# Two VectorE operands of layer 1 read from PSUM instead of SBUF

## The chip, the cores and the metric

The kernel runs on one core of one Trainium2 chip. The metric is the device time of one execution in microseconds. Five engines run side by side, each through its own list of instructions in order: TensorE (PE), VectorE (DVE), ScalarE (ACT), GpSimd (POOL) and SyncE (SP). They meet only at semaphores. TensorE writes its results to PSUM, which has eight banks of 512 fp32 values in each of 128 partitions; VectorE and ScalarE read and write PSUM and SBUF.

## What is computed

A graph with 6250 nodes (256 values each) and 100000 edges goes through two layers. Layer 0 sends a message along each edge, sums the messages by node and updates the node by a gate; a layer norm follows. Layer 1 is graph attention with 8 heads:

```python
    s_u = x @ W_u.T + b_u
    s_v = x @ W_v.T
    e = s_u[src] + s_v[dst]
    e = jnp.where(e >= 0, e, 0.2 * e)
    m = jax.ops.segment_max(e, dst, num_segments=n_nodes)
    e_exp = jnp.exp(e - m[dst])
    denom = jax.ops.segment_sum(e_exp, dst, num_segments=n_nodes)
    probs = e_exp / denom[dst]
    xh = x.reshape(n_nodes, head_dim, num_heads)
    msg = xh[src] * probs[:, None, :]
    out = jax.ops.segment_sum(msg, dst, num_segments=n_nodes)
```

The edges come sorted by `dst`. A second layer norm ends the computation.

## The kernel before

The kernel has five stages, one after the other: setup (some 320 us), layer 0 (to about 2900 us), the node update (to about 3200 us), layer 1 (to about 4845 us) and the output. The change lies in layer 1 alone, the function `layer1_phase`.

Layer 1 lays the edges out in 880 tiles of 128 edges, one edge to a partition, and takes them in 55 groups of 16 tiles (`GROUP` = 16). Two buffer sets (`SETS` = 2, index `r`) alternate. For group `g` the steps are these:

- GpSimd gathers the rows of the 16 tiles with 16 indirect DMAs (L1466), each of 128 rows of 264 fp32 values (`XW`: 256 features and 8 scores), into `feats[r]`. Their row numbers stand in `gsrc[r]` in SBUF. Before a group's gathers GpSimd waits for `index_ready`, and before each four of them until the sums that use the buffer are done (`agg_done`).
- VectorE forms the scores when all 16 gathers have landed and the sums of the group before are added (`take_scores`, L1589 to L1592), and then a running maximum along the edges (`local_max`, L1598 to L1601). Its last instruction in the body of a group is `stage_index` (L1574), which writes the row numbers of the group after the next into `gsrc[r]` and so releases that group's gathers.
- In the body of the next group VectorE first makes the one-hot tile of the nodes (`find_node`, L1578), chains the maxima over the tiles (L1659 to L1670), and compares in `find_edge` (L1581) a row of column numbers, `K["column"]`, broadcast over 16 tiles, with each edge's place, `loX`, broadcast over 128 columns. The result is `same`, 128 by 2048 values, the matrix that TensorE sums with. After two scans (L1679, L1680) and a turn on TensorE comes `below`, the score less its maximum (L1688).
- ScalarE takes the exponential of `below` (L1564) and writes the 8 weights of each edge into the last 8 columns of its row of `feats[r]`, where TensorE sums them with the features.
- VectorE multiplies the features by the weights in four quarters, in place (L1699). TensorE multiplies `same` with `feats` for two tiles at a time into `psU` (L1532), and VectorE adds each of the eight results to `acc` in SBUF (`add_sums`, L1611).

The order of each engine's work is written out by hand. On VectorE the body of a group is: L1578, the chain of maxima, L1581, the scans, L1688, L1693 (`acc` by a factor), two quarters of L1699 and the sums between and after the other two, then `take_scores` and `local_max` of the group after it, then L1574. In PSUM the stage has seven tensors of one bank each: `psE`, `psM`, `psV` and four `psU`. Layer 0 has the same kinds of work in other shapes: gathers at L918, scatters at L935, a comparison of two SBUF tensors at L1071, and at L1122 a sum of a PSUM tensor and an SBUF tensor.

## Time and profile before

| | us |
|---|---|
| median of 3 runs | 4930.07 (4929.89 to 4938.38) |
| the profiled execution | 4929.81 |
| its span in the trace | 4928.1 |
| POOL busy in the span | 3434.9 (70%) |
| PE busy | 3099.3 (63%) |
| DVE busy | 2202.6 (45%) |
| ACT busy | 908.4 (18%) |

The page gives the busy time in 40 slices of the span, one digit for each, in tenths:

```profile
PE   3547877777777777877778768834444444444441
DVE  2543333333333333333333349855555555555554
POOL 4238888888888888888888867756666666666564
PEclk9869898888998888888898889956666666666665
```

The last 14 slices are layer 1 and the output. No engine is full there: GpSimd is busy six tenths of the time, VectorE five, TensorE four.

### The profile page before, as it was taken

The numbers are of one execution on the slowest core, as the hardware profiler recorded it, in microseconds if no ns is written. First come the engines' busy times: TensorE is split into PE (matmuls) and PEld (weight loads), VectorE is DVE, ScalarE is ACT, GpSimd is POOL, SyncE is SP. The second block draws the span as 40 slices with busy tenths as digits, with TensorE's granted clock in tenths as the row PEclk, the third lists the DMA queues.
The fourth block names the chain that finished last, engine by engine and source line by source line (L and its number), as shares of the span: only waits on it lengthen the run. The fifth ranks groups of instructions, "written<-read, shape, count | busy, mean of one in ns | idle before, by whom it ended". The sixth has DMA issues, their size and how long they took to land. (4 is left out here: it accounts for less than half of the span.)

```text
span 4928.1 us, 61408 instructions
## 1 busy us (share of the span) xinstructions
PE 3099.3 (63%) x13554; PEld 1900.6 (39%) x13555; DVE 2202.6 (45%) x5019; ACT 908.4 (18%) x2810; POOL 3434.9 (70%) x2948
## 2 busy tenths in 40 slices
PE   3547877777777777877778768834444444444441
PEld 1224444444444444444444435523333333333331
DVE  2543333333333333333333349855555555555554
ACT  0212222222222222222222223300000000000002
POOL 4238888888888888888888867756666666666564
PEclk9869898888998888888898889956666666666665
DMA  7777767667767677677677666643333333333332
GB/s 285 193 241 137 135 126 136 133 123 135 132 126 138 127 131 134 126 135 132 123 136 132 123 133 206 181 148 93 95 92 100 93 94 91 96 98 94 92 93 66
DMA packets 471760, 641.52 MB, mean 130 GB/s; under 512 B 173608, under 2 KB 365636, under 8 KB 467887
## 3 DMA queue, kind: packets, MB, share of 16 engines
q0 software_dynamic: 198144, 339.26, 36.4%
q1 hardware_dynamic: 245994, 254.83, 17.6%
q10 hardware_dynamic: 27588, 47.08, 3.0%
q8 instruction: 10, 0.16, 0.0%
q14 instruction: 24, 0.19, 0.0%
HBM read 448.23 MB, written 192.71 MB: 130 GB/s over the span
## 5 line engine op out<-in xcount | busy, mean ns | idle before, releaser
L935 POOL DMA_INDIRECT S<-l_msum,l_sink x784 | 1280.7, 1634 | 254.2 <-issue 213.5
L1466 POOL DMA_INDIRECT l_feats<-X_rows,l_gsrc x880 | 1008.1, 1146 | 605.6 <-DVE l_gsrc L1574 340.7
L918 POOL DMA_INDIRECT l_ga<-A_rows,l_gsrc x784 | 791.3, 1009 | 265.6 <-issue 155.4
L1008 PE MATMUL l_psU<-l_hid,l_same 128*128 128x257 f32 x1568 | 585.0, 458 | 534.7 <-ACT l_hid L1044 518.2
L981 PE MATMUL l_psC<-l_table,l_onehot 128*128 x4728 | 726.5, 295 | 0.0
L1532 PE MATMUL l_psU<-l_feats,l_same 128*128 128x264 f32 x1760 | 555.7, 481 | 146.5 <-DVE l_feats L1699 129.2
L1048 ACT COPY l_msum<-l_psU 128x257 f32<-128x257 f32 x784 | 292.6, 373 | 1883.8 <-POOLq L934 1296.1
L974 PE MATMUL l_psC<-W1cT,l_attrT 64*128 64x256 f32 x1576 | 619.0, 476 | 13.1 <-DMA l_table<-B_rows 13.1
L981 PEld LDWEIGHTS l_psC<-l_table,l_onehot 128*128 128x128 bf16 x4728 | 426.0, 104 | 364.9 <-issue 303.4
L1008 PEld LDWEIGHTS l_psU<-l_hid,l_same 128*128 128x128 f32 x1568 | 266.1, 213 | 669.9 <-ACT l_hid L1044 598.9
L1532 PEld LDWEIGHTS l_psU<-l_feats,l_same 128*128 128x128 f32 x1760 | 413.8, 242 | 281.8 <-issue 189.2
L1122 DVE TENSOR_TENSOR l_hidden<-l_psG,bgate 128x256 f32<-128x256 f32 x147 | 62.4, 425 | 824.8 <-PE l_psG L1023 673.4
L974 PEld LDWEIGHTS l_psC<-W1cT,l_attrT 64*128 64x128 f32 x1576 | 260.3, 206 | 267.4 <-issue 230.7
L1080 DVE TENSOR_SCALAR l_togo<-srcT,spare 128x8 f32 x98 | 25.7, 262 | 694.9 <-POOLq L934 626.2
L1044 ACT ACTIVATE l_hid<-l_ga 128x256 f32<-128x256 f32 x784 | 331.0, 422 | 0.0
L1097 DVE TENSOR_TENSOR l_ga<-l_ga,l_psC 128x256 f32<-128x256 f32 x784 | 308.5, 415 | 45.0 <-PE l_psC L981 20.8
L1501 PE MATMUL l_psE<-ident,l_score 128*128 128x128 f32 x55 | 25.9, 471 | 435.4 <-DVE l_score L1592 435.4
L1611 DVE TENSOR_TENSOR acc<-acc,l_psU 128x264 f32 x440 | 188.4, 428 | 237.7 <-PE l_psU L1532 144.1
L1699 DVE TENSOR_TENSOR l_feats<-l_feats 128x1024 f32<-128x1024 f32 x220 | 264.0, 1221 | 4.2 <-DVE acc L1693 0.5
L1562 ACT ACTIVATE l_shrink<-l_psE 128x8 f32<-128x8 f32 x55 | 9.7, 177 | 1223.6 <-PE l_psE L1519 1042.8
L1023 PE MATMUL l_psG<-WhhT,l_xgT 128*128 128x256 f32 x588 | 195.4, 417 | 0.0
L1501 PEld LDWEIGHTS l_psE<-ident,l_score 128*128 128x128 f32 x55 | 9.9, 180 | 457.9 <-DVE l_score L1592 457.9
(346 smaller groups left out, 3512.2 us busy)
## 6 DMA issues: line engine op xcount, KB each, us to landing
l_srcb<-src_rows SPq DMA_DIRECT2D x99, 512.0 KB
l_locb<-lo_rows SPq DMA_DIRECT2D x55, 512.0 KB
S<-su_zeros ACTq DMA_DIRECT2D x24, 1156.5 KB
l_locb<-loc_rows SPq DMA_DIRECT2D x99, 256.0 KB
nd_sums<-S SPq DMA_DIRECT2D x196, 128.5 KB, 2.2
l_attr<-in_edge_attr SPq DMA_DIRECT2D x98, 256.0 KB
GH_rows<-l_hidden SPq DMA_DIRECT2D x49, 384.0 KB
nd_hidden<-GH_rows SPq DMA_DIRECT2D x49, 384.0 KB, 3.2
```

The costliest lines, as they stand in the source:

```text
L918: pool.indirect_dma_start(ga[:, s, :], None, D["A"], bass.IndirectOffsetOnAxis(ap=gsrc[h][:, j % HALF:j % HALF + 1], axis=0)).then_inc(gat ...
L935: pool.indirect_dma_start(D[f"S{j % NTAB}"], bass.IndirectOffsetOnAxis(ap=sink[j // HALF][:, j % HALF:j % HALF + 1], axis=0), msum[:, j % ...
L974: nc.tensor.matmul(pc(j), attrT[j // 4 % 2][side, j % 4 // 2 * P:(j % 4 // 2 + 1) * P], K["W1cT"][side, :], start=True, stop=False)
L981: t = nc.tensor.matmul(pc(j), onehot[j // HALF % 2][:, w, j % HALF, :], flat(table[:, bass.ds(blocks[j % 4] + w, 1), n * H:(n + 1) * H]), ...
L1008: nc.tensor.matmul(psU[j % 2][:, 0:UW], same[j // HALF][:, j % HALF, :], hid[:, j % RING, :], start=True, stop=True).then_inc(agg_done, 1)
L1023: t = nc.tensor.matmul(psG[:, 0:H], xgT[:, k * P:(k + 1) * P], K["WhhT"][:, k, n * H:(n + 1) * H], start=(k == 0), stop=(k == HC - 1))
L1044: nc.scalar.activation(hid[:, j % RING, 0:H], ga[:, j % SLOTS, :], ACT.Relu).then_inc(hid_ready, 1)
L1048: nc.scalar.copy(msum[:, j % RING, :], psU[j % 2][:, 0:UW]).then_inc(msum_ready, 1)
L1097: nc.vector.tensor_tensor(ga[:, s, :], ga[:, s, :], pc(j), ALU.add).then_inc(pre_ready, 1)
L1466: pool.indirect_dma_start(feats[r][:, t, :], None, D["X1"], bass.IndirectOffsetOnAxis(ap=gsrc[r][:, t:t + 1], axis=0)).then_inc(gathered[r ...
L1532: i = nc.tensor.matmul(psU[n % 4][:, 0:XW], same[:, t, :], feats[r][:, t, :], start=(t % PAIR == 0), stop=(t % PAIR == PAIR - 1))
L1699: nc.vector.tensor_tensor(f3, f3, w3, ALU.mult).then_inc(weighted, 1)
```

## The change

A new PSUM tensor `psW` takes the eighth bank. Two things lie in it. The first 128 columns, `weight`, hold the weights of a group, and the next 128, `column`, hold the row of column numbers, copied there once before the loop. `find_edge` reads its first operand from `column` in PSUM; its second, `loX`, stays in SBUF. ScalarE takes the exponential twice: first into `weight` (which signals `weights_ready`), then into the rows of `feats` as before (which signals the new semaphore `weights_in_rows`). VectorE's four products read the weights from PSUM and the features from SBUF. TensorE waits for `weights_in_rows` before the group's sums. The place of `stage_index` is the same as before, last in the body.

```diff
--- before.py
+++ after.py
@@ -1388,6 +1388,7 @@
         psE = m.ps("psE", [P, 512])
         psM = m.ps("psM", [P, 512])
         psV = m.ps("psV", [P, 512])
+        psW = m.ps("psW", [P, 512])
         psU = [m.ps(f"psU{q}", [P, 512]) for q in range(4)]
         keys_in, tables_ready, table_split = m.sem("keys_in"), m.sem("tables_ready"), m.sem("table_split")
         loc_in = [m.sem(f"loc_in{r}") for r in range(SETS)]
@@ -1399,12 +1400,14 @@
         ends_ready, ends_turned = m.sem("ends_ready"), m.sem("ends_turned")
         carries_ready, carries_turned, shrink_ready = m.sem("carries_ready"), m.sem("carries_turned"), m.sem("shrink_ready")
         max_ready, max_turned = m.sem("max_ready"), m.sem("max_turned")
-        below_ready, weights_ready = m.sem("below_ready"), m.sem("weights_ready")
+        below_ready, weights_ready, weights_in_rows = m.sem("below_ready"), m.sem("weights_ready"), m.sem("weights_in_rows")
         weighted, agg_done, acc_done = m.sem("weighted"), m.sem("agg_done"), m.sem("acc_done")
         dve_step, pool_waited = m.sem("dve_step"), m.sem("pool_waited")
         block = st.enter_context(nc.Block())
 
         ENDS, CARRY, SHRINK = P, P + 2 * GROUP, P
+        weight = psW[:, 0:GROUP * NH].rearrange("p (t h) -> p t h", h=NH)
+        column = psW[:, P:2 * P]
 
         def groups(engine, body):
 
@@ -1522,6 +1525,7 @@
                 pe.wait_ge(max_ready, g + 1)
                 nc.tensor.transpose(psM[:, 0:P], top[:, :], K["ident"][:, :]).then_inc(max_turned, 1)
                 pe.wait_ge(same_ready, g + 1)
+                pe.wait_ge(weights_in_rows, g + 1)
                 for n in range(PAIRS):
                     if n % 2 == 0:
                         pe.wait_ge(weighted, g * 4 + (n // 2 + 1))
@@ -1561,7 +1565,8 @@
                 act.wait_ge(carries_turned, g + 1)
                 nc.scalar.activation(shrink[:, :], psE[:, SHRINK:SHRINK + NH], ACT.Exp).then_inc(shrink_ready, 1)
                 act.wait_ge(below_ready, g + 1)
-                nc.scalar.activation(feats[r][:, :, H:XW], below[:, :, :], ACT.Exp).then_inc(weights_ready, 1)
+                nc.scalar.activation(weight, below[:, :, :], ACT.Exp).then_inc(weights_ready, 1)
+                nc.scalar.activation(feats[r][:, :, H:XW], below[:, :, :], ACT.Exp).then_inc(weights_in_rows, 1)
                 if not isinstance(g, int) or g < XG - SETS:
                     act.wait_ge(sv_done, g + 1)
                     stage_window(g + SETS, r)
@@ -1578,7 +1583,7 @@
                 nc.vector.tensor_scalar(onehot[:, :, :], locb[r][:, :, :], K["winid"][:, 0:1], None, ALU.is_equal).then_inc(onehot_ready, 1)
 
             def find_edge(g):
-                nc.vector.tensor_tensor(same[:, :, :], K["column"][:, :].unsqueeze(1).to_broadcast([P, GROUP, P]),
+                nc.vector.tensor_tensor(same[:, :, :], column.unsqueeze(1).to_broadcast([P, GROUP, P]),
                                         K["loX"][:, bass.ds(g * GROUP, GROUP)].unsqueeze(2).to_broadcast([P, GROUP, P]),
                                         ALU.is_equal).then_inc(same_ready, 1)
 
@@ -1627,6 +1632,7 @@
             split_float(nc, first_steps, K["svf"][:, :, :], svrest[:, :, :],
                         [table[:, :, n * NH:(n + 1) * NH] for n in range(NSPLIT)])
             dve.sem_inc(table_split, 1)
+            nc.vector.tensor_copy(column, K["column"][:, :])
             nc.vector.memset(ones[:, :], 1.0)
             nc.vector.memset(forth[:, 0:1], LOW)
             nc.vector.memset(carry[:, 1, GROUP - 1:GROUP], LOW)
@@ -1693,9 +1699,8 @@
                     c.link(nc.vector.tensor_tensor(rows, rows, factor[:, :].unsqueeze(1).to_broadcast([P, XW // NH, NH]), ALU.mult))
                 dve.wait_ge(weights_ready, g + 1)
                 for q in range(4):
-                    f = feats[r][:, q * QUARTER:(q + 1) * QUARTER, :]
-                    f3 = f[:, :, 0:H].rearrange("p t (c h) -> p t c h", h=NH)
-                    w3 = f[:, :, H:XW].unsqueeze(2).to_broadcast([P, QUARTER, H // NH, NH])
+                    f3 = feats[r][:, q * QUARTER:(q + 1) * QUARTER, 0:H].rearrange("p t (c h) -> p t c h", h=NH)
+                    w3 = weight[:, q * QUARTER:(q + 1) * QUARTER, :].unsqueeze(2).to_broadcast([P, QUARTER, H // NH, NH])
                     nc.vector.tensor_tensor(f3, f3, w3, ALU.mult).then_inc(weighted, 1)
                     if q == 1 or q == 2:
                         add_sums(g, (2 * q - 2, 2 * q - 1), blocks, first)
```

## Rows read from the trace of the kernel before

**Rows 1.** The waits of 3300 to 4800 us: who waited, for whom, total us, times, longest.
```profile
DVE l_score L1589 <- DMA l_feats<-X_rows,l_gsrc: 308.5, 52, 7.9
POOL l_feats L1466 <- DVE l_gsrc L1574: 304.9, 52, 6.1
```

**Rows 2.** The gathers of layer 1 by their line (ns min/median/max), and their row of the page.
```profile
L1466 POOL DMA_INDIRECT l_feats<-X_rows,l_gsrc x880: 940/946/3010, 3214.5 to 4820.3; - x176
...
L1466 POOL DMA_INDIRECT l_feats<-X_rows,l_gsrc x880 | 1008.1, 1146 | 605.6 <-DVE l_gsrc L1574 340.7
```

**Rows 3.** The timeline of one group: start us, duration us, engine, line, idle before it.
```profile
4010.09 0.17 DVE L1574 CAST l_gsrc<-srcX 128x16 int32 x1
...
4011.18 1.02 POOL L1466 DMA_INDIRECT l_feats<-X_rows,l_gsrc  x1 [5.84 <-DVE l_gsrc L1574]
...
4013.09 2.27 DVE L1581 TENSOR_TENSOR l_same<-column,loX 128x2048 f32<-128x2048 f32 x1
...
4013.75 2.44 POOL L1466 DMA_INDIRECT l_feats<-X_rows,l_gsrc  x1 [0.30 <-issue]
...
4017.68 0.29 DVE L1688 TENSOR_TENSOR l_below<-l_score,l_psM 128x128 f32<-128x128 f32 x1 [0.77 <-PE l_psM L1523]
4017.78 0.94 POOL L1466 DMA_INDIRECT l_feats<-X_rows,l_gsrc  x1 [0.31 <-issue]
...
4018.00 0.31 ACT L1564 ACTIVATE l_feats<-l_below 128x128 f32<-128x128 f32 x1 [3.28 <-DVE l_below L1688]
4018.41 2.36 DVE L1699 TENSOR_TENSOR l_feats<-l_feats 128x1024 f32<-128x1024 f32 x2
...
4019.03 1.43 POOL L1466 DMA_INDIRECT l_feats<-X_rows,l_gsrc  x1 [0.30 <-issue]
...
4021.93 0.43 DVE L1611 TENSOR_TENSOR acc<-acc,l_psU 128x264 f32 x1 [1.16 <-issue]
4022.01 0.95 POOL L1466 DMA_INDIRECT l_feats<-X_rows,l_gsrc  x1 [0.30 <-issue]
...
4036.14 0.56 DVE L1589 TENSOR_REDUCE l_score<-l_psV 128x128 f32<-128x384 f32 x1 [4.95 <-DMA l_feats<-X_rows,l_gsrc]
```

**Rows 4.** Busy time of two bursts of 16 gathers: the second one and one later.
```profile
core 0: us, PE busy (x) PEld busy (x) DVE busy (x) ACT busy (x) POOL busy (x), PEclk, DMA share, GB/s
3235.67:3255.38 19.71, 0.58 (x16) 0.51 (x16) 10.84 (x1) 4.46 (x17) 15.11 (x16) 0.50 0.88 280
4011.15:4034.18 23.03, 12.86 (x53) 9.70 (x53) 13.74 (x29) 1.99 (x10) 18.43 (x16) 0.65 0.40 113
```

**Rows 5.** Timeline: the first and the last comparison with a gather under it.
```profile
3285.24 2.27 DVE L1581 TENSOR_TENSOR l_same<-column,loX 128x2048 f32<-128x2048 f32 x1
...
3285.44 2.88 POOL L1466 DMA_INDIRECT l_feats<-X_rows,l_gsrc  x1 [0.30 <-issue]
...
4799.05 2.27 DVE L1581 TENSOR_TENSOR l_same<-column,loX 128x2048 f32<-128x2048 f32 x1
4799.18 2.97 POOL L1466 DMA_INDIRECT l_feats<-X_rows,l_gsrc  x1 [0.30 <-issue]
```

**Rows 6.** Timeline of layer 0: L1122, a gather under it; then all gathers of L918 (min/median/max).
```profile
2284.39 0.42 DVE L1122 TENSOR_TENSOR l_hidden<-l_psG,bgate 128x256 f32<-128x256 f32 x1 [4.58 <-PE l_psG L1023]
2284.61 0.99 POOL L918 DMA_INDIRECT l_ga<-A_rows,l_gsrc  x1 [0.30 <-ACT l_msum L1048]
...
L918 POOL DMA_INDIRECT l_ga<-A_rows,l_gsrc x784: 942/987/1980, 322.8 to 2864.2; - x196
```

**Rows 7.** VectorE groups by line, 3300 to 4800 us, and one line of the nodes stage.
```profile
L1699 DVE TENSOR_TENSOR l_feats<-l_feats 128x1024 f32<-128x1024 f32 x204 | 244.8, 1221 | 3.2
L1611 DVE TENSOR_TENSOR acc<-acc,l_psU 128x264 f32 x411 | 175.9, 428 | 222.2 <-PE l_psU L1532 130.6 <-issue 69.6 <-DVE acc L1611 21.5
...
L1693 DVE TENSOR_TENSOR acc<-acc,l_factor 128x264 f32 x51 | 22.1, 434 | 0.0
...
L1308 DVE TENSOR_TENSOR nd_rz<-nd_psRZ,nd_addend x49: 677/681/692, 2919.8 to 3197.5; 128x512 f32<-128x512 f32 x49
```

**Rows 8.** Timeline of GpSimd alone: the pause after the first gather of a burst.
```profile
4043.25 1.41 POOL L1466 DMA_INDIRECT l_feats<-X_rows,l_gsrc  x1 [2.25 <-issue]
```

## The prediction

> **What bounds the kernel now.** The change touches layer 1 alone, so I read the waits of that stretch first. Two waits answer each other there: VectorE waits for the gathers (308.5 us before L1589), and GpSimd waits for the row numbers of L1574 (304.9 us) [rows 1]. So the stage is one ring. GpSimd issues 16 gathers, the last one lands, VectorE forms the scores and the local maxima and writes the next row numbers, and GpSimd starts again. The timeline of one group shows GpSimd idle for 5.84 us between two bursts, and VectorE idle for 4.95 us until the burst has landed, with all its own work on the group done [rows 3]. Neither engine is full, but each us that a burst grows is a us of the ring. The wait for `agg_done` inside a burst never holds: the pauses between gathers are 0.30 us almost everywhere [rows 3].
>
> Next the burst itself. The smallest gather takes 940 ns and the median 946 ns, but the mean is 1146 ns and the longest 3010 ns [rows 2]. The second burst ran while VectorE did nothing with two SBUF tensors. It held 15.11 us of gathers in 19.71 us, which is 16 times 0.945 and 15 pauses. A later burst held 18.43 us of gathers in 23.03 us: all of its extra 3.3 us lies inside gathers [rows 4]. Summed over the 880 gathers, 1008.1 - 880 x 0.946 = 175.6 us lie above the median [rows 2]. That is the pot from which the change can take.
>
> The timelines show when a gather grows. One that started 0.66 us after the comparison L1581 took 2.44 us and ended 0.83 us after it. The first and the last such gather took 2.88 and 2.97 us and ended 0.81 and 0.83 us after the comparison [rows 3, 5]. One that started under the first of two products (L1699, 2.36 us for the two) took 1.43 us and ended 0.83 us after the first [rows 3]. So a gather that starts while such an instruction runs is held near its beginning, until the instruction has ended. Under L1611 (`acc` from SBUF, `psU` from PSUM, result to SBUF) a gather that started 0.08 us in took 0.95 us, and under L1688 (`score` from SBUF, `psM` from PSUM) one took 0.94 us [rows 3]. L1581 and L1699 read two tensors from SBUF; L1611 and L1688 read one. All bursts look alike: going through the 880 gathers in the timeline, I count 53 that start under L1581, with 67.5 us above the median together, and 136 that are held by L1699, with 97.5 us. None of those that start under L1611 or L1688 is above it. The other 10.6 us lie under setup work, under L1578, L1659 and L1680 (0.04 us at each of the 53 starts under it), and in scatter.
>
> **The change part by part.**
>
> *Removed: the hold under L1699.* After the change it reads features from SBUF and weights from PSUM, which is the form of L1611. Gain 97.5 us by the rows of L1611, nothing if PSUM did not help. I take 97.5.
>
> *Removed: the hold under L1581.* Here the first operand moves to PSUM and the second stays in SBUF. The nearest row is L1122 of layer 0, first operand `psG`, second an SBUF tensor. A gather that started 0.22 us into it took 0.99 us, and 987 ns is the median of all L918 gathers [rows 6]. So the order of operands does not matter, though L1122 is short (0.42 us). Gain 67.5 us; nothing at the other end. I take 67.5.
>
> *Moved reads: the length of the two VectorE instructions.* No row shows a product of 1024 or a comparison of 2048 values with a PSUM operand. L1611 takes 428 ns for 264 values, and L1693, the same size with both inputs in SBUF, 434 ns; L1308, first operand in PSUM and second in SBUF, takes 681 ns for 512 [rows 7]. From L1611 to L1308 that is 253 ns for 248 values, the rate of L1699 (1221 ns for 1024). I take the same length. The bounds are a few ns less and twice the time per value, which is rival three.
>
> By the Trainium skill (VectorE: DVE Perf Modes, The TRN2 errata) a PSUM source costs 120 cycles against 58 at 0.96 GHz. That would be 0.06 us more for each of five instructions of a group, 0.3 us that VectorE's idle time covers, and the pair of L1611 and L1693 does not show it [rows 7].
>
> *Added on ScalarE: a second exponential of each group.* It takes 0.31 us as L1564 does [rows 3]; written to PSUM, the first could take 0.05 us less or more, since no row shows ScalarE writing there. Products wait for the first alone. L1564 runs beside L1693, which ends at about the same time, so VectorE sees nothing of a small difference. The second ends some 0.35 us later, under the first product (1.22 us), and TensorE waits for that product anyway: cost zero, or 0.3 us of TensorE per group without that cover, which is not in the ring either. Behind the second exponential ScalarE's window copies (L1552) move by 0.35 us. They serve the group after the next, a whole period later. Cost zero.
>
> *Added: the wait for `weights_in_rows` on TensorE.* Queued behind it are the sums, which `weighted` holds for longer. Zero. *Added: one copy of 128 columns before the loop,* under 0.3 us. No DMA, no SP work and no GpSimd instruction is added or moved, and L1574 stays where it is.
>
> *What is late next.* VectorE idles 308.5 / 52 = 5.9 us per group before L1589 [rows 1]. The bursts shrink by 165 / 53 = 3.1 us each, so 2.8 us stay on average, and 4.95 - 3.3 = 1.6 us in the group shown. GpSimd still sets the pace: each us taken from a burst arrives.
>
> *New holds.* With the long holds gone, starts fall at fixed 1.25 us steps from the start of the burst, and may meet the short instructions that still read two SBUF tensors. By the group shown none meets L1693, whose 0.43 us would cost at most 0.43 - 0.12 = 0.31 us. The scan L1680 is met now already, for 0.04 us. If both were met at their start in all 53 groups it would cost 53 x (0.31 + 0.36) = 35 us.
>
> *Sum.* The profiled execution took 4929.81 us, its span 4928.1, and the median of the runs is 4930.07, so the three agree. 4929.8 - 97.5 - 67.5 = 4764.8 us.
>
> **The rivals.**
>
> *One: the comparison keeps its hold,* because its second operand still comes from SBUF. Then 4929.8 - 97.5 = 4832 us. Against it: L1122 [rows 6]. For it: L1122 is short, and such starts are few.
>
> *Two: nothing is given back.* The hold would hang on the length of the instruction or on its writing to SBUF, not on its second input. Then 4930 us. Against it: L1611 writes to SBUF and holds nothing [rows 3]. By the Trainium skill (SBUF — State Buffer, Who interferes with whom) an earlier probe saw no stall of GpSimd's DMAs under `tensor_tensor`, since descriptor generation is inferred to need the write interface only, and that would give this case; the same section says that two SBUF inputs contend with a GpSimd instruction that reads SBUF. The trace bears out the second: gathers of 2.44 us under L1581 [rows 3].
>
> *Three, the other side: PSUM operands stream at half rate,* as broadcast operands that are read again and again. Then L1581 grows by 2.13 us and the four products by 4 x 1.07 = 4.27 us, 6.4 us on VectorE per group. The ring passes to VectorE from 2.8 us on, and the kernel is slower from 5.9 us on. 53 x (6.4 - 5.9) = 27 us: 4957 us. Against it: L1611 and L1308 [rows 7], though neither broadcasts its PSUM operand.
>
> *Four: only the products slow down so.* 4.27 - 2.8 = 1.5 us per group, 53 x 1.5 = 78 us: 4843 us. VectorE is then the bound.
>
> **How the numbers follow.** Forecast 0.80, rival one 0.07, two 0.05, three 0.04, four 0.04. The forecast's range: upward 35 us of new holds, to 4800. Downward the whole pot, 175.6 us, and the pause of 2.25 us in place of 0.30 that 8 of the bursts have after their first gather [rows 8], 8 x 1.95 = 16 us, if that too hangs on VectorE: 4738. So 4740 to 4800 holds 0.80. Faster by over 0.2% (about 10 us, what a measurement of this kernel can tell from no change): 0.80 + 0.07 + 0.04 = 0.91. Within it 0.05, slower 0.04.
>
> **What would show it.** Gathers of L1466 in layer 1 at a mean near 0.96 us instead of 1.146, the longest under 1.5 us, and the mean period of a group near 26.0 us (29.1 less 3.1), where the 52 steps from the first to the last comparison give (4799.05 - 3285.24) / 52 = 29.1 [rows 5]. VectorE's wait before L1589 near 2.8 us per group and still ended by the gathers' DMA. L1581 at 2.27 us and the product at 1.22 us. Wrong would be: gathers still near 2.4 us under L1581 (rival one), L1581 above 3 us (three), or VectorE without idle time before L1589 (four).

## The result and the profile after

The changed kernel is slower: 5139.52 us median (5128.53 to 5145.09, four runs) against 4930.58 us (4929.89 to 4938.38) before, a ratio of 1.0415 with a 95% interval from 1.0396 to 1.0433. The forecast was 4764.8 us. The profiled execution took 5128.53 us and its span is 5126.8 us, so that is the time to explain: 198.7 us more than before.

The page of the changed kernel: its 40 slices, two of its DMA queues, and three rows of its costliest groups (out<-in, count | busy us, mean ns | idle us before).

```profile
PE   2657778787777778787777687344444444444441
...
DVE  3543333333333333333333398554544554555445
...
POOL 3248888888888888888888677444444444444444
PEclk9878988888888888888988899556666666666665
...
q8 instruction: 10, 0.16, 0.0%
q14 instruction: 23, 0.19, 0.0%
...
L1469 POOL DMA_INDIRECT l_feats<-X_rows,l_gsrc x880 | 837.5, 952 | 971.1 <-DVE l_gsrc L1579 706.0
...
L1616 DVE TENSOR_TENSOR acc<-acc,l_psU 128x264 f32 x440 | 188.5, 428 | 751.7 <-DMA B_rows<-su_zeros 317.3
...
L1704 DVE TENSOR_TENSOR l_feats<-l_feats,l_psW 128x1024 f32<-128x1024 f32 x220 | 263.0, 1216 | 2.3 <-ACT l_psW L1568 0.3
```

Layer 1's loop has grown longer, so it fills more slices, and in these VectorE is at 0.4 to 0.5. The gathers are as forecast: 837.5 us where there were 1008.1 [rows 2], a mean of 952 ns. Their line and that of the comparison (ns min/median/max) say the same:

```profile
L1469 POOL DMA_INDIRECT l_feats<-X_rows,l_gsrc x880: 943/949/1372, 3214.7 to 5015.3; - x176
...
L1586 DVE TENSOR_TENSOR l_same<-l_psW,loX x55: 2271/2292/2293, 3264.5 to 5026.6; 128x2048 f32<-128x2048 f32 x55
```

The median gather is as before and the longest takes 1372 ns in place of 3010 [rows 2]. The comparison takes 2292 ns and the product 1216 ns, as they did before [rows 3, 7]. Everything that the change was to do, it did. The gain of 170.6 us in the gathers is there, and the kernel is 199 us slower. The waits of the 52 steps (3300 to 5000 us) show where:

```profile
POOL l_feats L1469 <- DVE l_gsrc L1579: 669.2, 52, 14.1
...
PE l_psU L1536 <- DVE l_feats L1704: 422.8, 105, 9.3
DVE acc L1616 <- DMA B_rows<-su_zeros: 312.5, 64, 8.0
DVE acc L1616 <- PE l_psU L1536: 264.0, 140, 6.0
...
DVE acc L1616 <- issue: 128.0, 78, 7.4
...
PE l_psU L1536 <- issue: 100.1, 31, 5.6
```

GpSimd used to wait 304.9 us for the row numbers [rows 1], 5.9 us for each group. It now waits 669.2 us, 12.9 for each. VectorE's wait for the gathers' DMA before the score reduction (308.5 us in rows 1) is gone: after the start of the loop, L1594 waits for nothing. So the ring's slack is used up, and VectorE sets the pace. Its own idle time has moved to L1616, the addition of the sums, and the releasers that stand there make no sense: `su_zeros` belongs to a stage long over, and "issue" means that the profile knows of nothing to wait for. The timeline of one group (start us, duration us, engine, line, idle before it) shows what happens:

```profile
4009.21 0.95 POOL L1469 DMA_INDIRECT l_feats<-X_rows,l_gsrc  x1 [13.19 <-DVE l_gsrc L1579]
...
4017.37 6.35 PE L1536 MATMUL l_psU<-l_feats,l_same 128*128 128x264 f32 x16 [2.49 <-DVE l_feats L1704]
...
4019.53 0.43 DVE L1616 TENSOR_TENSOR acc<-acc,l_psU 128x264 f32 x1 [1.16 <-issue]
...
4027.32 0.43 DVE L1616 TENSOR_TENSOR acc<-acc,l_psU 128x264 f32 x1 [7.35 <-issue]
4027.66 1.21 DVE L1704 TENSOR_TENSOR l_feats<-l_feats,l_psW 128x1024 f32<-128x1024 f32 x1
4028.01 0.95 POOL L1469 DMA_INDIRECT l_feats<-X_rows,l_gsrc  x1 [0.30 <-issue]
...
4029.00 3.88 PE L1536 MATMUL l_psU<-l_feats,l_same 128*128 128x264 f32 x8 [5.28 <-DVE l_feats L1704]
4032.24 0.43 DVE L1616 TENSOR_TENSOR acc<-acc,l_psU 128x264 f32 x1 [3.36 <-PE l_psU L1536]
...
4040.99 1.02 POOL L1469 DMA_INDIRECT l_feats<-X_rows,l_gsrc  x1 [12.02 <-DVE l_gsrc L1579]
```

The burst begins at 4009.21. At 4019.53 VectorE adds the first pair of sums, and then it does nothing for 7.35 us. The block of 16 matmuls that began at 4017.37 holds four pairs of sums, and TensorE finished the second at 4021.25. Nothing that the program asks for is missing, and yet the next addition starts at 4027.32. The third product follows it at 4027.66, so TensorE, which needs that product, has idled for 5.28 us when it goes on at 4029.00; VectorE adds again at 4032.24, after 3.36 us, although this pair too lay in the block that ended at 4023.72. That is 23.03 us after the burst began, and from there on nothing is late. The last gather started at 4028.01. The row numbers come so late that the next burst starts at 4040.99, after 12.02 us of waiting where there were 5.84 [rows 3].

To count this in every kernel the same way I take, for each addition of a pair, its start less the later of two ends: that of VectorE's instruction before it, and that of TensorE's last matmul of the pair. Where this is above 1 us it is a *stall*. Before: none. After: 102, with 461.5 us, among 440 additions. The last stall of a group ends 23.0 us after the burst began in nearly every group.

VectorE is not alone. The register steps of the loop on ScalarE (ACTq) and SyncE (SPq), which wait for no semaphore, take this long (ns min/median/max):

```profile
L1556 ACTq FUSED_REGOPS  x440: 3/138/1422, 3239.5 to 4972.7; - x147
...
L1427 SPq FUSED_REGOPS  x26: 55/700/728, 3218.8 to 4875.0; - x26
```

From 3300 us on, no register step of either engine in the kernel before took 0.5 us or more; here some 250 do, nearly all of them 0.7 us, mostly at 1.40 us from one to the next. TensorE is touched too: where it had idled ahead of its sums for no known reason for 2.4 us in all, it now does so for 100.1 us, 5.6 us at the longest. And it runs its sums at a lower clock.

The kernel before shows the same on ScalarE once, in the second burst of the stage, where VectorE did nothing with two SBUF tensors and so no gather was held [rows 4]. ScalarE's register steps (one line, whole execution) and its copies in that burst:

```profile
L1552 ACTq FUSED_REGOPS  x440: 15/132/704, 3238.8 to 4776.2; - x147
...
3248.07 0.21 ACT L1552 COPY l_window<-l_table 128x24 bf16 x1 [3.92 <-issue]
3248.20 0.95 POOL L1466 DMA_INDIRECT l_feats<-X_rows,l_gsrc  x1 [0.30 <-issue]
3249.45 0.95 POOL L1466 DMA_INDIRECT l_feats<-X_rows,l_gsrc  x1 [0.30 <-issue]
3249.47 0.21 ACT L1552 COPY l_window<-l_table 128x24 bf16 x1 [1.19 <-issue]
...
3250.87 0.21 ACT L1552 COPY l_window<-l_table 128x24 bf16 x1 [1.19 <-issue]
```

These copies come at 1.40 us, and ahead of each stands a step of ScalarE's sequencer of 0.69 or 0.70 us. Seven such steps of L1552 lie between 3242 and 3256 us. No tensor of the change exists in that kernel.

The windows of one block of the changed kernel's sums and of the stage (busy us of PE, PEld, DVE, ACT and POOL, granted clock, DMA share, GB/s):

```profile
4017.40:4023.70 6.30, 6.30 (x16) 4.63 (x16) 1.40 (x2) 0.80 (x4) 4.77 (x6) 0.59 0.52 147
3300.00:4800.00 1500.00, 689.86 (x2549) 485.74 (x2548) 756.22 (x1644) 100.50 (x495) 690.47 (x726) 0.63 0.29 83
```

While these 16 matmuls ran the granted clock was 0.59 of full speed, where the sums of the group in rows 3 had 0.72 between 4019.8 and 4030.5 us. Over the stage it is 0.63 against 0.66. These are mixtures of the engine's two levels, 1.2 and 2.4 GHz; ahead of this block TensorE had idled for 2.49 us. The mean matmul of the sums, within 3300 to 4800 us, went from 481 to 558 ns.

### The profile page after: what moved, and what is told of

It is laid out like the page before. It is cut to its first block and busy times, and to the rows that moved or that the text cites. A ratio compares the mean times of both kernels' runs of the same rounds, so it can differ in the third digit from the quotient of the medians.

```text
span 5126.8 us, 61518 instructions
## 1 busy us (share of the span) xinstructions
PE 3213.0 (63%) x13554; PEld 1965.6 (38%) x13555; DVE 2208.0 (43%) x5020; ACT 922.0 (18%) x2865; POOL 3265.5 (64%) x2948
## 5 line engine op out<-in xcount | busy, mean ns | idle before, releaser
L1469 POOL DMA_INDIRECT l_feats<-X_rows,l_gsrc x880 | 837.5, 952 | 971.1 <-DVE l_gsrc L1579 706.0
L1536 PE MATMUL l_psU<-l_feats,l_same 128*128 128x264 f32 x1760 | 670.5, 554 | 535.6 <-DVE l_feats L1704 429.9
L918 POOL DMA_INDIRECT l_ga<-A_rows,l_gsrc x784 | 791.9, 1010 | 265.7 <-issue 162.2
L1536 PEld LDWEIGHTS l_psU<-l_feats,l_same 128*128 128x128 f32 x1760 | 477.4, 281 | 709.0 <-issue 575.7
L1616 DVE TENSOR_TENSOR acc<-acc,l_psU 128x264 f32 x440 | 188.5, 428 | 751.7 <-DMA B_rows<-su_zeros 317.3
L1122 DVE TENSOR_TENSOR l_hidden<-l_psG,bgate 128x256 f32<-128x256 f32 x147 | 62.5, 425 | 824.2 <-PE l_psG L1023 625.9
L1704 DVE TENSOR_TENSOR l_feats<-l_feats,l_psW 128x1024 f32<-128x1024 f32 x220 | 263.0, 1216 | 2.3 <-ACT l_psW L1568 0.3
L1071 DVE TENSOR_TENSOR l_same<-l_srcb,srcT 128x1024 f32<-128x1024 f32 x99 | 121.1, 1223 | 141.6 <-PE l_psU L1008 139.8
L1023 PEld LDWEIGHTS l_psG<-WhhT,l_xgT 128*128 128x128 f32 x588 | 124.2, 211 | 21.1
```

The lines of the kernel that those rows point to most:

```text
L918: pool.indirect_dma_start(ga[:, s, :], None, D["A"], bass.IndirectOffsetOnAxis(ap=gsrc[h][:, j % HALF:j % HALF + 1], axis=0)).then_inc(gat ...
L1023: t = nc.tensor.matmul(psG[:, 0:H], xgT[:, k * P:(k + 1) * P], K["WhhT"][:, k, n * H:(n + 1) * H], start=(k == 0), stop=(k == HC - 1))
L1469: pool.indirect_dma_start(feats[r][:, t, :], None, D["X1"], bass.IndirectOffsetOnAxis(ap=gsrc[r][:, t:t + 1], axis=0)).then_inc(gathered[r ...
L1536: i = nc.tensor.matmul(psU[n % 4][:, 0:XW], same[:, t, :], feats[r][:, t, :], start=(t % PAIR == 0), stop=(t % PAIR == PAIR - 1))
L1704: nc.vector.tensor_tensor(f3, f3, w3, ALU.mult).then_inc(weighted, 1)
```

## The experiments

Theory A is that the gathers themselves, now unbroken at 1.25 us from start to start, hold up the other engines' instruction handling, and that the holds which the change removed had been the gaps in which the others came through. Theory B is that something the change adds is at fault: the PSUM operands, the second exponential or the new wait. Theory C is that bandwidth is short: the gathers' packets or the other loads press together. Where an experiment changed the kernel by more than a few lines only its core is shown. Each was run beside the kernel before, which took 4925.7 us (e1 to e4), 4932.8 (e5 to e12) and 4938.1 (e13 to e15, the median of seven runs). A time without an interval is one run. In the expectations S is theory A, P and I are the operands and the added instructions of theory B, and L is a part of theory C. R is a narrower form of A: something serves the gathers one by one at a fixed rate, and the others wait until none is left.

**e3: all added instructions, no gap removed.** The weights and the column lie in SBUF tiles, and the rest of the change stays.

```diff
-        psW = m.ps("psW", [P, 512])
-        weight = psW[:, 0:GROUP * NH].rearrange("p (t h) -> p t h", h=NH)
-        column = psW[:, P:2 * P]
+        weight_sb, column_sb = m.sb("weight_sb", [P, GROUP, NH]), m.sb("column_sb", [P, P])
+        weight, column = weight_sb[:, :, :], column_sb[:, :]
```

> The changed kernel with all its instructions and waits, but weight and column lie in SBUF, so both comparison and products read two SBUF tensors again. Three theories of why the changed kernel loses 210 us: (S) 16 gathers in an unbroken row at 1.25 us each starve the other engines of instructions, and the holds that the two-SBUF-operand instructions put into the burst had been the breaks that let them through; (P) the PSUM operands or the bank psW cost it; (I) the added instructions and the added wait cost it. S: holds are back (mean gather 1.14 us), no stall, 4930 us within 10. P: the same, 4930. I: about 5130 us, with gathers at a mean of 1.14 us.

Measured: 4937.1 us, gathers at 1146 ns, a burst of 23.26 us, a period of 29.11 us and no stall: the kernel before in every row. The time lies within the 4925.7 to 4941.2 us that runs of the kernel before took. So the second exponential, the copy and the wait for `weights_in_rows` cost nothing that shows, as the prediction had it, and theory B keeps only the PSUM operands.

**e4: the PSUM operands, with gaps put back.** GpSimd fills 1024 values ahead of gathers 4, 8 and 12, which makes each of these pauses 1.5 us longer. Nothing else differs from the changed kernel.

```diff
                     if t % QUARTER == 0:
+                        if t:
+                            nc.gpsimd.memset(idle[:, 0:1024], 0.0).then_inc(paused, 1)
+                            pool.wait_ge(paused, g * 3 + t // QUARTER)
```

> The changed kernel, with three fillings of 1024 values on GpSimd in each burst (before gathers 4, 8 and 12), each of which GpSimd waits for: some 1 to 1.3 us of pause each, about as much as the holds had taken. S: the stalls of VectorE and TensorE vanish or shrink, 4900 to 4990 us although GpSimd has more to do. P and I: the stalls stay and the pauses come on top or hide, 5130 to 5200 us.

Measured: 4996.8 us. GpSimd is given 4.4 us more to do in each burst (24.43 us against 20.05), and the kernel is 132 us *faster* than the changed one. There is no stall, with both operands in PSUM. So the PSUM operands alone bring no stall, and the stalls come and go with the gaps between gathers. One question is left: do unbroken gathers do this only beside PSUM operands? For ScalarE the second burst of the kernel before says no. For VectorE's additions no run tells, since two operands in SBUF would hold the gathers again.

**e1 and e2: one half of the change each.** e1 keeps only the comparison's column in PSUM, e2 only the weights.

```diff
 e1
-                    w3 = weight[:, q * QUARTER:(q + 1) * QUARTER, :].unsqueeze(2).to_broadcast([P, QUARTER, H // NH, NH])
+                    f = feats[r][:, q * QUARTER:(q + 1) * QUARTER, :]
...
+                    w3 = f[:, :, H:XW].unsqueeze(2).to_broadcast([P, QUARTER, H // NH, NH])
 e2
-                nc.vector.tensor_tensor(same[:, :, :], column.unsqueeze(1).to_broadcast([P, GROUP, P]),
+                nc.vector.tensor_tensor(same[:, :, :], K["column"][:, :].unsqueeze(1).to_broadcast([P, GROUP, P]),
```

> The kernel before with the comparison's row alone in PSUM; products read two SBUF tensors. S: holds of the products break the burst at about gathers 6, 9 and 11, few or no stalls, 4860 to 4950 us; my forecast's own account without any stall would give 4930 - 67.5 = 4862. P: if the bank or the PSUM operand of the comparison is the cost, 5000 us or more. I: 4862.

> The changed kernel with the comparison reading two SBUF tensors again; only the products read PSUM. S: one hold near the start of a burst (gather 1 or 2), then 13 or 14 gathers unbroken: the stalls stay, 5050 to 5200 us. P: a smaller loss if it is the comparison's operand, the whole if it is the products'. I: about 5130, as the added exponential and wait are still in.

Measured: e1 4926.2 us, gathers at 1069 ns, bursts of 21.99 us, 78 stalls with 185.8 us. e2 4940.1 us, 1027 ns, 21.29 us, 111 stalls with 363.4 us. Each half takes its own hold away and each brings stalls, which give back about what it gained. For e2 5050 us or more had been expected, so the cost was missed by over 100 us. In e2 no register step of ScalarE or SyncE takes 0.5 us after 3300 us, although VectorE stalls for 363.4 us: long register steps and stalls need not come together. The two halves together lose far more than their sum; that the second half meets a ring without slack is my reading, and no run shows it.

**e5: a pause that is no pause.** 16 values before each gather but the first.

```diff
                     gather(r, t)
...
+                    if t:
+                        pool.wait_ge(paced, g * (GROUP - 1) + t)
+                        pool.sem_inc(pool_waited, 1)
+                        nc.gpsimd.memset(idle[:, 0:16], 0.0).then_inc(paced, 1)
```

> The changed kernel with one filling of 16 values on GpSimd ahead of each gather but the first of a burst: some 0.1 to 0.4 us more per gather. The gathers of the changed kernel follow each other at 1.25 us; its stalls end 23.0 us after the start of the burst in nearly every group, and ScalarE and SyncE step at 1.40 us inside them. (R) Something serves a gather in 1.40 us, so a queue grows while gathers come at 1.25, and the other engines wait until it has served all 16 (16 x 1.40 = 22.4 us). Then a pace of 1.40 us or more leaves no queue: no stalls, and 4930 us or less where the pace is between 1.40 and 1.45. (S, a break of a us is needed for the others to get through): an even pace without breaks doesn't help, stalls stay, 5100 us or more.

Measured: 5131.7 us, stalls of 441.6 us. The filling ran within the 0.30 us that lie between two gathers anyway: the step from gather to gather was 1.26 to 1.27 us, so the experiment did not change what it was to change. It does show that more instructions and waits on GpSimd alone do no harm.

**e6, e7, e8: is it bytes?** In all three the loop leaves out a part of the data. e6 loads the row of window numbers for one partition instead of 128. e7 gathers 132 of each row's 264 values. e8 gathers 64 of 128 rows.

```diff
 e6
-                sp.dma_start(locb[r][:, :, :].rearrange("p t e -> p (t e)"),
+                sp.dma_start(locb[r][0:1, :, :].rearrange("p t e -> p (t e)"),
 e7
-                pool.indirect_dma_start(feats[r][:, t, :], None, D["X1"],
+                pool.indirect_dma_start(feats[r][:, t, 0:XW // 2], None, D["X1"],
 e8
-                pool.indirect_dma_start(feats[r][:, t, :], None, D["X1"],
-                                        bass.IndirectOffsetOnAxis(ap=gsrc[r][:, t:t + 1], axis=0)).then_inc(gathered[r], 16)
+                pool.indirect_dma_start(feats[r][0:64, t, :], None, D["X1"],
+                                        bass.IndirectOffsetOnAxis(ap=gsrc[r][0:64, t:t + 1], axis=0)).then_inc(gathered[r], 16)
```

> The changed kernel, where SyncE's load of the edge positions inside the loop fills one partition instead of 128 (4 KB of DMA for 512 KB), so the node comparison works on old data from the third group on; everything else stays. (L) The stalls start just behind this load, when its DMA and the gathers share the queues, and the load is their cause: without it no stalls, about 4765 us, the forecast's time. (R) or (S): the load has no part in it, 5050 to 5150 us.

> The changed kernel, where each gather of the loop fetches 132 instead of 264 values per row: the same number of rows and instructions, half the bytes. The other half of the features and the scores are then old. If the bytes that the gathers move cause the stalls (DMA queues), they vanish: about 4765 us. If the number of rows or of GpSimd's instructions causes them, nothing changes: 5130 us.

> The changed kernel, where each gather of the loop fetches 64 rows instead of 128: half the rows and half the bytes, the same number of instructions; half of the edges are then old. If each row's descriptors cause the stalls, they shrink or vanish (4765 us or less, as a gather may get shorter too). If the number of instructions counts, and their pace gets faster, they stay.

Measured: 5110.7, 5104.1 and 5138.6 us, stalls of 435.5, 433.2 and 471.7 us, and the last stall of a group typically ends 22.9, 22.9 and 22.8 us after the burst began. Bytes, packets and rows hardly matter, and theory C falls with that. e8 is the telling one: its gathers are shorter (909 ns) and its bursts too (19.07 us), and the stalls grow. What counts is the number of gather instructions, as far as these runs tell.

**e10: 14 gathers instead of 16.** The loop leaves out the rows of the last two in each group.

```diff
-                for t in range(GROUP):
+                for t in range(14):
```

> The changed kernel with 14 gathers in each group instead of 16; the last two tiles of a group are left out (zeros). (R): the stalls end when the queue of 14 is served, 14 x 1.40 + 0.6 = 20.2 us after the start of the burst instead of 23.0, and the time falls by about 52 x 2.8 = 145 us to 4990. (S) or a cause on VectorE's or TensorE's own side: the end of the stalls stays where it is, 22.9 us, or lies elsewhere, and 5100 to 5130 us.

Measured: 4984.1 us; stalls of 329.8 us. The timeline of one burst:

```profile
3520.49 0.94 POOL L1469 DMA_INDIRECT l_feats<-X_rows,l_gsrc  x1 [13.61 <-DVE l_gsrc L1579]
...
3536.73 0.95 POOL L1469 DMA_INDIRECT l_feats<-X_rows,l_gsrc  x1 [0.30 <-issue]
3537.10 0.43 DVE L1616 TENSOR_TENSOR acc<-acc,l_psU 128x264 f32 x1 [5.86 <-DMA B_rows<-su_zeros]
...
3540.73 0.43 DVE L1616 TENSOR_TENSOR acc<-acc,l_psU 128x264 f32 x1 [2.07 <-DMA B_rows<-su_zeros]
```

The last stall ends 20.24 us after the burst began, and 20.25 to 20.35 us is typical. Two gathers fewer end it 2.75 us earlier: 1.375 us for each, although a gather is issued every 1.25 us. So I tried this rule: each gather instruction hands over 1.375 us of work when it ends, this is worked off in order, and the other engines' instruction handling gets its turn only when none is left. The first gather ends after 0.95 us: 0.95 + 16 x 1.375 = 22.95 us (measured 23.0), and with 14, 20.2 us (20.25). As the rule was made from these two, they don't test it. In the kernel before it leaves about 2.3 us of each burst free, since a gather that is held hands over nothing in the meantime; in the changed one about 0.25.

**e9 and e14: a slower pace.** As e5, but with 216 and 368 values, which bring the usual step from gather to gather to 1.41 and 1.54 us.

> As the evenly paced kernel, whose filling of 16 values hid in the 0.30 us pause between gathers and so paced them at 1.27 us, with fillings of 216 values (some 0.30 us by the fillings of 16 and of 1024 values), so a gather comes each 1.42 us, with no longer break anywhere. (R, something serves a gather in 1.40 us): no queue, no stalls, burst 22.3 us, period 28.2 us instead of 29.1 before, 4885 to 4895 us. (S, breaks of near a us are needed): stalls of VectorE stay and the time is above 5100 us.

> As the kernel with a gather each 1.42 us, with fillings of 368 values: a gather each 1.55 us. Model so far: each gather hands 1.375 us of work to something, beginning as the gather ends, and the other engines are let through only when none is left; this gave the end of the stalls at 0.95 + 16 x 1.375 = 22.95 us (measured 23.0), with 14 gathers 20.2 (20.25), and at 1.42 us 0.95 + 15 x 1.417 + 1.375 = 23.6 (23.65). At 1.55 us a gap of 0.17 us is left behind each gather: stalls over 1 us in few groups or none, burst 24.3 us, period 30.1 us, 4985 us. If only breaks of near a us let the others through, stalls of several us per group stay, ending near 0.95 + 15 x 1.55 + 1.375 = 25.6 us, and 5000 to 5060 us.

Measured: e9 4953.2 us. Stalls of 330.3 us remain, and they end typically at 23.65 us; the end of the last gather's work by the rule is 15 x 1.41 + 0.95 + 1.375 = 23.5. But by the rule as it stands each gather's work is done before the next one ends, so there should be no stall, and none was expected (4885 to 4895 us). Gaps of 1.41 - 1.375 = 0.04 us seem to let too little through; the rule has no term for that. Yet the kernel is 175 us faster than the changed one, though its bursts last 2.4 us longer. e14, where each gap is 0.17 us, came as expected: 4989.0 us (4985 expected), and not one stall, not even above 0.5 us. Its waits (3300 to 4600 us; engine, line, waited for: us, times, longest):

```profile
DVE l_score L1600 <- DMA l_feats<-X_rows,l_gsrc: 295.5, 43, 8.8
POOL l_feats L1470 <- DVE l_gsrc L1585: 250.9, 43, 5.9
...
DVE acc L1622 <- PE l_psU L1542: 138.3, 161, 1.6
```

VectorE waits for the gathers' DMA again, 6.9 us for each group (295.5 / 43), and GpSimd for the row numbers 5.8 us: the ring is as in rows 1, with bursts of 24.34 us. No register step takes 0.5 us any more. Each burst is 4.3 us longer than in the changed kernel (20.05 us), and that costs less than the stalls it prevents. A pace between 1.41 and 1.54 us was not tried.

**e13: what of VectorE is stuck?** 16 tiny fillings on VectorE right behind the first addition of a group, with no semaphore between.

```diff
                     nc.vector.tensor_tensor(rows, rows, psU[n % 4][:, 0:XW], ALU.add).then_inc(acc_done, 1)
+                    if n == 0:
+                        for k in range(16):
+                            nc.vector.memset(tiny[:, k:k + 1], 0.0)
```

> The changed kernel, with 16 fillings of one value on VectorE behind the first of the eight sums of each group, without any semaphore between them; each takes about 0.06 us. They stand where the stalls begin. (F, the instructions themselves don't arrive while the queue of gathers is being served): the fillings stop in the middle, with pauses of 0.7 us or several us between two of them that wait for nothing. (W, only waits on semaphores are slow to be answered): all 16 run through in about 1 to 2 us in every group, and the stall comes at the wait behind them. Either way the time is within 15 us of the changed kernel, 5130.

Measured: 5136.7 us. The same group, in its timeline:

```profile
4019.37 0.43 DVE L1617 TENSOR_TENSOR acc<-acc,l_psU 128x264 f32 x1 [1.16 <-issue]
4019.75 0.28 DVE L1620 MEMSET l_tiny<- 128x1 f32 x16
...
4021.37 0.43 DVE L1617 TENSOR_TENSOR acc<-acc,l_psU 128x264 f32 x1 [1.34 <-PE l_psU L1537]
...
4021.72 1.21 DVE L1708 TENSOR_TENSOR l_feats<-l_feats,l_psW 128x1024 f32<-128x1024 f32 x1
...
4030.51 0.43 DVE L1617 TENSOR_TENSOR acc<-acc,l_psU 128x264 f32 x1 [7.58 <-DMA B_rows<-su_zeros]
```

All 16 ran in 0.28 us, and so they did in every group, as TensorE's 16 matmuls did above. The stall of 7.58 us stands before a later addition, one with register steps and a wait ahead of it. My reading is that the engine itself is free and runs what it already holds, and that what is late is what its sequencer has to do. Whether that is the arrival of instructions or the answers to waits this run doesn't tell. The register steps of ScalarE and SyncE speak against the answers alone, since they wait for nothing and take 0.70 us.

**e11, e12, e15: cut the ring instead.** `stage_index`, which writes the row numbers for the group after the next and stands last in a group's work, goes to its beginning: e11 and e15 in the kernel before, e12 in the changed one.

```diff
             def body(g, r, first, last):
...
+                if not isinstance(g, int) or g < XG - SETS:
+                    stage_index(g + SETS, r)
                 if not last:
                     find_node
...
-                if not isinstance(g, int) or g < XG - SETS:
-                    stage_index(g + SETS, r)
```

> The kernel before, where VectorE writes the index list of the group after the next as the first instruction of a group's body instead of the last. The ring of burst, landing, scores and index list is cut: GpSimd can start the next burst as soon as it is done with the last one. GpSimd has 23.25 us of burst per group (with its holds) and VectorE 23.2 us of work. Period 24 to 25.5 us, 4670 to 4740 us, if nothing stalls. (R): gathers come at 1.45 us on average, slower than 1.40, so hardly a stall. (S): holds are in, no stall either.

> The changed kernel with the same early index list. Without holds GpSimd could deliver 16 gathers in 20 us. (R): gathers would come at 1.25 us and the queue grow, and since bursts now follow each other, VectorE would be stalled over and over; the ring through the sums (a gather waits until its buffer's sums are done) then holds the period at 23 us or more, 24 to 29: 4650 to 4920. It is slower than the kernel before with the same early list, by R as by S.

> The kernel before with the index list written first in a group's body, timed: 4688 us in one look, so a ratio of 0.951 to the kernel before, within 0.003.

Measured: e11 4687.9 us and e12 5075.0 us. e15 is the same kernel as e11: with e11's run four runs, median 4691.73 us (4682.69 to 4704.0), against 4938.11 us (4931.58 to 4941.15, seven runs): a ratio of 0.9509 with an interval from 0.9491 to 0.9526. It beats both kernels. e11's wait of VectorE before the scores (3300 to 4580 us), its gathers, and what GpSimd waited for ahead of them (us, times):

```profile
DVE l_score L1589 <- DMA l_feats<-X_rows,l_gsrc: 25.6, 18, 3.7
...
L1466 POOL DMA_INDIRECT l_feats<-X_rows,l_gsrc x880: 942/949/3060, 3218.4 to 4578.4; - x176
...
  issue: 262.1, 811
  PE l_psU L1532: 58.4, 56
  DVE l_gsrc L1574: 10.0, 11
```

The wait for the row numbers is 10.0 us in all, where it was above 300 us [rows 1]. The period fell from 29.11 to 24.56 us, though gathers are held more than ever (their mean is 1175 ns, the longest 3060). GpSimd now sets the pace: its bursts, holds included, fill 23.80 of the 24.56 us, so the holds still cost time. Hardly a stall is left: 11 with 24.2 us in e11's trace, none in e15's. In e12 there are no stalls at the additions, but VectorE waits elsewhere, most of it before L1683 (376.9 us), and GpSimd waits 624.9 us for TensorE's sums. Counted as at the additions, 47 of the 55 L1683 start over 1 us after the matmuls of L1520 that they need and the VectorE instruction ahead are done, 380.6 us together: the same trouble, before another instruction. For e12 4650 to 4920 us had been expected; that it would be slower than e11 came true, by 387 us. The same edit is worth 245 us with the operands in SBUF and 54 to 70 us with them in PSUM (5075.0 against 5128.5 to 5145.1).

## Why the prediction was wrong

**The holds: right.** Removing both was put at 165 us; the gathers' sum fell by 170.6 us, 1008.1 to 837.5. Rivals one and two, that a hold would stay, are out: the longest gather of the stage is 1372 ns. By the Trainium skill (SBUF — State Buffer, Who interferes with whom) a VectorE instruction with at most one SBUF input, outside the 2-port modes, does not contend with GpSimd. The trace after agrees: 99 gathers start under L1586 and 163 under L1704, and the longest of them takes 958 ns.

**The lengths with a PSUM operand: right.** 2292 ns against 2273 before, and 1216 against 1221. Rivals three and four, half rate, are out.

**The added instructions: right.** With all of them in, e3 took 4937.1 us, within what runs of the kernel before took.

**What is late next: the step that failed.** The prediction took 3.1 us from each burst, found 2.8 us of VectorE's idle time left and concluded that "each us taken from a burst arrives". Bursts did shrink by 3.2 us (23.25 to 20.05). But the step took everything else in the group to go on as before, and TensorE, VectorE, ScalarE and SyncE did not: with the gathers unbroken VectorE's additions alone stood still for 461.5 us. GpSimd's wait for the row numbers grew from 5.9 to 12.9 us of each group, and VectorE's for the gathers went to nothing, so VectorE set the pace and no us taken from a burst arrived. In whole periods it closes: 32.92 against 29.11 us over 52 steps are 198 us. How these split is only an estimate. The slack that the step counted, 53 x 2.8 = 148 us, could take up that much, and 461.5 - 148 = 313 us would be left on the path: 4929.8 - 170.6 + 313 = 5072 us, 56 us short. TensorE's slower sums (558 ns a matmul against 481) are the largest other thing seen. The same sum for e1 takes 67 us from 4925.7, finds slack for all its 185.8 us of stalls and gives 4858; 4926.2 was measured. So the terms of the loss, other than the stalls themselves, stay open.

**The rivals: none was this one.** Slower had a chance of 0.04, all of it by a slower VectorE. The rival on the other side had VectorE become the bound, and so it did, but by another cause: it was to be busy longer, and in truth it idled, 751.7 us before L1616 against 237.7 before. The range had downward room for still fewer holds and upward room for new ones; no term of it asked what the holds had been good for. The trace of before had something to see it by: the burst that the prediction took as its picture of unheld gathers, 3235.67 to 3255.38 us [rows 4], is the one in which ScalarE's register steps take 0.70 us and its copies come at 1.40 us. Had the prediction read the other engines in that window, it would have had the mechanism, though hardly its size. VectorE's idle time before L1611 that stands as "issue" [rows 7] is no such sign: measured from the end of TensorE's pair, no addition of that kernel starts even 0.6 us late. In the range, 8 bursts were counted with a long pause after the first gather; the trace has seven, which moves the lower bound by 2 us.

**New holds: none of size came.** The 35 us kept for them were not needed: the whole stage holds about 837.5 - 880 x 0.949 = 2.4 us above the median.

**The comparison with what would show it.** The gathers' mean (0.952 for "near 0.96"), their longest, L1586 and L1704 came as written. The period did not (32.9 for 26.0), nor did the wait of 2.8 us before the scores, which came to 0. That was written down as the sign of VectorE being the bound, and it was.

## What to carry to other kernels

Before taking a stall away, ask what runs in it. A queue that is issued without a gap can starve engines that share no data with it, and then some filling between its entries is a gain (5128.5 us without, 4953.2 with 0.16 us more from gather to gather). And where two engines wait for each other, look first for the step that closes the ring: moving the row numbers to the front of the group brought 4.9% with every hold in place. Taking the holds away lost time with the ring closed (4.15%) and with it cut (387 us, e12 against e11).

## What the runs showed of the hardware

- Gathers that follow each other at 1.25 us hold up the instruction handling of the other engines. Each weighs about 1.375 us, independently of its bytes (e7) and nearly of its rows (e8); at a pace of 1.54 us (e14) no stall is left. The figure of 1.375 is worked out from e10 and the changed kernel. e14 agrees with the rule; e9 does not, and the rule does not order e1 and e2 rightly, where by it about 0.9 and 1.3 us of a burst are free and 185.8 and 363.4 us are stalled. Where in the burst a gap lies must matter too; that was not tried.
- What it is that they share stays open. It isn't the bytes moved (e6, e7: 435.5 and 433.2 us of stalls).
- Not everything is held up: within such a stretch 16 fillings ran in 0.28 us and 16 matmuls in 6.35 us, while a register step on SyncE takes 0.70 us. That instructions already queued run on fits this, but is a reading.
- On ScalarE it needs no operand of VectorE in PSUM: in the second burst of the kernel before, where no gather was held, ScalarE's register steps took 0.69 to 0.70 us.
- By the Trainium skill (SBUF — State Buffer, Who interferes with whom) "PE and ACT never wait on anyone". Of the SBUF ports no run here says otherwise, but it doesn't say what unbroken gathers of GpSimd can do to TensorE and ScalarE in another way: TensorE idled for up to 5.6 us with nothing known to wait for, and ScalarE's register steps reached 1422 ns.
- By the Trainium skill (Runtime: NRT & Kernel Launch, Instruction fetch mechanics) a sequencer fetches its instructions by a DMA queue of its own, in blocks of 16 KiB. The trace after has two queues of the kind "instruction". The ten packets of one carry 0.16 MB, which is 16 KiB each; the 23 of the other are of half that size or less. None of either lies between 3370 and 5003 us, where nearly all the stalls are, so it is not block fetches that the gathers delay here, as far as the trace tells.
